# A four-stage graph network on one core: message layers written out with deeper load rings, and one scaled table between the first two layers

## What is computed

```python
h = relu(layernorm(x)); x = x + L0(h)     # conv:  relu(segment_sum((h @ W * norm)[src], dst) * norm + b)
h = relu(layernorm(x)); x = x + L1(h)     # sage:  concat([h, scaled mean of h[src] and h]) @ W1 + b
h = relu(layernorm(x)); x = x + L2(h)     # attention over edges and own edge, batch norm
h = relu(layernorm(x)); x = x + L3(h)     # three typed layers:
#   m = where(etype == 0, h @ W[0], h @ W[1])[src]
#   h = act(segment_sum(m, dst) + h @ Ws + b)      relu, relu, none
```

## Time and profile before

| | us |
|---|---|
| median of the runs (three) | 6772.4 |
| profiled execution | 6746.68 |
| its span | 6745.1 |
| conv layer (545 to 1346 us of the span) | 801 |
| sage layer (1346 to 2145) | 799 |
| attention stages (2145 to 4518) | 2373 |
| typed layers (4518 to 6745), three of 742 to 743 | 2227 |

### The profile page before, as it was taken

One profiled execution on the slowest core, in us unless ns is written; L12 is line 12 of the kernel. 1 busy time (PEld: TensorE's weight loads), 2 busy tenths in 40 slices (PEclk: granted clock), 3 DMA queues, 4 the chain that ended last, 5 costly groups with the idle time before them and its releaser, 6 DMA issues. The chain is left out here.

```text
span 6745.1 us, 89039 instructions
## 1 busy us (share of the span) xinstructions
PE 4393.0 (65%) x26272; PEld 3765.7 (56%) x26272; DVE 3539.0 (52%) x9258; ACT 2200.7 (33%) x5554; POOL 2825.2 (42%) x2867
## 2 busy tenths in 40 slices
PE   6502565546666787776659999415777477757777
PEld 5402555536655454554447777315777467656677
DVE  8862555624444565665579999762323223323333
ACT  6572544513333232232225444551111111111111
POOL 0014554255543677776500000025554455545553
PEclk9855666667777787887779999656777677777777
DMA  6033666645654222222222222343444344434444
GB/s 171 6 68 82 145 144 141 134 92 126 127 116 104 63 66 66 66 68 62 50 42 55 53 52 55 81 95 80 97 93 98 69 92 96 92 81 90 96 93 91
DMA packets 1695961, 589.73 MB, mean 87 GB/s; under 512 B 1606839, under 2 KB 1626102, under 8 KB 1695498
## 3 DMA queue, kind: packets, MB, share of 16 engines
q1 hardware_dynamic: 1189958, 380.24, 25.6%
q10 hardware_dynamic: 416196, 116.81, 7.7%
q0 software_dynamic: 89600, 90.32, 6.7%
HBM read 378.26 MB, written 222.06 MB: 89 GB/s over the span
## 5 line engine op out<-in xcount | busy, mean ns | idle before, releaser
L1944 POOL DMA_INDIRECT early<-node_g,src_w x1176 | 1141.7, 971 | 1036.1 <-DMA edge_h<-early 583.8
L1944 POOL DMA_INDIRECT l1ring<-node_g,src_w x392 | 373.5, 953 | 444.7 <-DMA edge_h<-l1ring 243.0
L1091 POOL DMA_INDIRECT fscat<-node_g,early x392 | 439.2, 1120 | 263.5 <-issue 114.3
L1206 DVE TENSOR_TENSOR fslz<-bank,fsy 128x512 f32<-128x512 f32 x448 | 267.0, 621 | 497.6 <-issue 290.9
L1944 POOL DMA_INDIRECT l0ring<-node_g,src_w x392 | 375.4, 958 | 346.2 <-DMA edge_h<-l0ring 219.8
L2604 POOL COPY x_sb<-fbxn 128x448 f32 x56 | 31.5, 562 | 1140.0 <-DVE fbxn L2663 1140.0
L1093 POOL DMA_INDIRECT fscat<-node_g,early x392 | 433.9, 1107 | 128.2 <-issue 128.2
L1182 ACT ACTIVATE fsy<-bank 128x512 f32<-128x512 f32 x448 | 242.3, 544 | 737.1 <-remote 234.6
L2021 PE MATMUL bank<-l0S,l0msg 128*128 128x128 f32 x1568 | 297.8, 366 | 146.2 <-issue 97.6
L1141 PE MATMUL bank<-Wlr,fscatT 128*128 128x256 f32 x784 | 273.1, 433 | 171.6 <-ACT fscatT L1173 147.6
L2021 PE MATMUL bank<-l1S,l1msg 128*64 128x128 f32 x1568 | 300.6, 312 | 124.8 <-issue 124.2
(11 more groups left out here) (328 smaller groups left out, 11365.2 us busy)
## 6 DMA issues: line engine op xcount, KB each, us to landing
node_g<-amax ACTq DMA_DIRECT2D x168, 224.0 KB
edge_h<-early SPq DMA_DIRECT2D x168, 224.0 KB
early<-node_g,src_w POOLq DMA_INDIRECT x1176
l0msg<-edge_a SPq DMA_DIRECT2D x56, 256.0 KB
l0msg<-edge_h SPq DMA_DIRECT2D x56, 256.0 KB
l1msg<-edge_h SPq DMA_DIRECT2D x56, 256.0 KB
alpha<-edge_h SPq DMA_DIRECT2D x56, 256.0 KB
l3win<-edge_h SPq DMA_DIRECT2D x56, 256.0 KB
```

Source lines behind the costliest of these rows:

```text
L1091: pool.indirect_dma_start(out=cat[:, s, t, 0:F], out_offset=None, in_=node_g, in_offset=bass.IndirectOffsetOnAxis(ap=src_i[:, col], axis=0 ...
L1206: v.tensor_tensor(lz[:, kind, t0:t1, :], z_bank(g)[:, 0:(t1 - t0) * HF].rearrange("p (t c) -> p t c", c=HF), y[:, g % 2, 0:t1 - t0, :], AL ...
L1944: pool.indirect_dma_start(out=ring[:, n % RING, t, :], out_offset=None, in_=table_in, in_offset=bass.IndirectOffsetOnAxis(ap=src_w[:, n * ...
```

## The change

It rewrites `layer`, and touches the plan of factors.

- Buffers: the gather ring has four slots in a typed layer (RING) and three otherwise; loaded rows have four buffers in a typed layer (DEEP) and three otherwise, instead of two. In conv and sage the ring now lies in the last third of the array `early`.
- SP's list: own rows (or edge attributes) of n + DEEP - 1 and the factors of n + 1 are asked for after the edge rows of n and the store of n + 2.
- One table between conv and sage: conv writes only the scaled rows. Sage uses them also for its own half and multiplies the product by the root that undoes the scale (`send_root`, one reciprocal at the start; one DVE operation more a window). The factors of sage are multiplied by the sending scale in the plan (`both`).
- PE, ACT and DVE are written out over the 56 windows, with one semaphore for each kind of step.
- DVE's order in a typed layer: matrices(n + 2), messages(n + 1), update(n).
- The last window gathers 6 tiles instead of 7, as the 392nd holds no edges.

The core of the diff (the waits of ACT and the index arithmetic that only follow the written-out loops are left out):

```diff
@@ plan
+                invr = tb("invr", [R, 2, NBLK * P]); both = tb("both", [P, T])
+                    pe.wait_ge(both_ok, 1)
-                        for k, of in enumerate((inv_cnt, upd_scale)):
+                        for k, of in enumerate((inv_cnt, both)):
+                    v.tensor_tensor(both[:, :], upd_scale[:, :], rs_send[:, :], ALU.mult).then_inc(both_ok, 1)
@@ layer
-                win = tb("win", [P, 2, WT, F]) if typed else None
-                msg = tb("msg", [P, 2, WT, M])
+                RING, DEEP = (4, 4) if typed else (3, 3)
+                ring = rows(ring_at, RING, HS)
+                win = rows(RING * HS * F, DEEP, WT) if typed else None
+                msg = tb("msg", [P, 2 if typed else DEEP, WT, M])
-                own = None if conv else tb("own", [P, 2, HS + 1, 2 * F if sage else F])
+                own = None if conv else tb("own", [P, DEEP, HS + 1, F])
-                RING = 3
@@ layer, gpsimd
-                        for t in range(HS):
+                        for t in range(real_tiles(n)):
@@ layer, sync
-                    def windows(n):
...
-                        if j > 0:
-                            sp.wait_ge(msg_ok[s] if typed else agg_ok[s], j)
-                            if typed:
-                                sp.wait_ge(agg_ok[s], j)
...
+                    def own_rows(n):
+                        if n >= DEEP:
+                            sp.wait_ge(agg_ok, n - DEEP + 1)
                         if conv:
...
+                        else:
+                            sp.dma_start(own[:, n % DEEP, 0:HS, :], tiles(table_in[nodes_of(n), :])).then_inc(own_in[n % DEEP], 16)
+
+                    def edge_rows(n):
+                        begin = begin_of(n)
+                        if n >= DEEP:
+                            sp.wait_ge(msg_ok if typed else agg_ok, n - DEEP + 1)
                         m = min(n + 1, NS - 1)
                         if n == 0:
                             sp.wait_ge(kept[0], 16)
                         sp.wait_ge(kept[m % RING], 16 * (m // RING + 1))
...
                     def factors(n):
+                        if n >= 2:
+                            sp.wait_ge(scaled, n - 1)
...
+                    for n in range(DEEP - 1):
+                        own_rows(n)
+                    if not typed:
+                        factors(0)
                     keep(0)
                     keep(1)
                     for n in range(NS):
+                        edge_rows(n)
                         if n + 2 < NS:
                             keep(n + 2)
-                        windows(n)
-                        if not typed and n >= 1:
-                            factors(n - 1)
-                    if not typed:
-                        factors(NS - 1)
+                        if n + DEEP - 1 < NS:
+                            own_rows(n + DEEP - 1)
+                        if not typed and n + 1 < NS:
+                            factors(n + 1)
@@ layer, tensor
                                 if sage:
-                                    nc.tensor.matmul(bank[2 * s + b][F:2 * F, col], own[:, s, t, F:2 * F], ident[:, :], start=True, stop=True)
-                                    nc.tensor.matmul(to, own[:, s, t, 0:F], ident[:, :], start=True, stop=False)
+                                    nc.tensor.matmul(bank[2 * s + b][F:2 * F, col], own[:, d, t, :], ident[:, :], start=True, stop=True)
+                                    nc.tensor.matmul(to, own[:, d, t, :], ident[:, :], start=True, stop=False)
...
+                    sums(0)
+                    for n in range(NS):
+                        if n + 1 < NS:
+                            sums(n + 1)
+                        products(n)
@@ layer, scalar
                             for t in range(HS):
-                                ins = A.activation(h[:, s, t, :], xn[:, s, t, :], ACT.Relu, bias=ln[:, s, 6, t:t + 1], scale=ln[:, s, 5, t:t + 1])
-                                if conv:
-                                    ins = A.activation(g[:, s, t, :], xn[:, s, t, :], ACT.Relu, bias=ln[:, s, 1, t:t + 1], scale=ln[:, s, 0, t:t + 1])
+                                ins = A.activation(h[:, s, t, :], xn[:, s, t, :], ACT.Relu, bias=ln[:, s, b, t:t + 1], scale=ln[:, s, m, t:t + 1])
...
-                                act.dma_start(tiles(node_h[at, :]), h[:, s, :, :]).then_inc(stored[s], 16)
-                                act.dma_start(tiles(table_out[at, :]), g[:, s, :, :]).then_inc(stored[s], 16)
+                            act.dma_start(tiles(table_out[at, :]), h[:, s, :, :]).then_inc(stored[s], 16)
@@ layer, vector
+                    if sage:
+                        v.reciprocal(send_root[:, :], rs_send[:, :])
...
+                    def messages(n):
+                        dve.wait_ge(rows_in[n % DEEP], 16 * (n // DEEP + 1))
+                        if n >= 2:
+                            dve.wait_ge(agg_ok, n - 1)
...
+                        v.tensor_tensor(o[:, s, :, :], po, wide((norm if conv else send_root)[:, tl]), ALU.mult).then_inc(o_free, 1)
+                        v.drain()
+                        v.tensor_tensor(o[:, s, :, :], o[:, s, :, :], rowb((b0 if conv else b1)[:, :]), ALU.add)
...
+                    matrices(0)
+                    matrices(1)
                     if typed:
+                        messages(0)
+                    for n in range(NS):
+                        if not typed:
+                            copied_sums(n)
+                        if n + 2 < NS:
+                            matrices(n + 2)
+                        if typed and n + 1 < NS:
+                            messages(n + 1)
+                        if typed:
+                            update(n)
+                        elif n >= 1:
+                            update(n - 1)
```

More of the change, by code:

```diff
@@ L1917, in layer @@
                 xn = lent(alpha, 2 * HS * F, lambda shape: tb("xn", shape)); h = lent(amax, 2 * HS * F, lambda shape: tb("h", shape))
-                g = tb("g", [P, 2, HS, F]) if conv else None
                 bs = tb("bs", [P, 2, HS, 6]); ln = tb("ln", [P, 2, 8, HS])
[L1920 to L1927, removed]
+                (S_ok, msg_ok, agg_ok, aT_ok, scaled, prod, o_free, x_ok, x_kept, var_ok, sd_ok, ln_ok, h_ok, padded, w_in) = (
+                    sm(n) for n in ("S_ok", "msg_ok", "agg_ok", "aT_ok", "scaled", "prod", "o_free", "x_ok", "x_kept", "var_ok", "sd_ok", "ln_ok", "h_ok", "padded", "w_in"))
+                gathered, kept = many("gathered", RING), many("kept", RING)
+                rows_in, own_in = many("rows_in", DEEP), many("own_in", DEEP)
+                inv_in, loop_out, stored = many("inv_in", 2), many("loop_out", 2), many("stored", 2)
                 PER = 16 * HS
-                RING = 3
-                rows_in = two("rows_in")
-                gathered, kept = ([sm(f"{name}{r}") for r in range(RING)] for name in ("gathered", "kept"))
-                ring = early_ring(RING) if typed else tb("ring", [P, RING, HS, F])
+                real_tiles = lambda n: min(HS, -(-N // P) - n * HS)
+                assert NS > RING and real_tiles(NS - 1) > 0
                 CH = [(0, 4), (4, HS)]
@@ L2048, in _ @@
                         pe.wait_ge(w_in, 32)
-                    sums(0, 0, True)
-                    def body(j, first, last):
-                        sums(j, 1, first)
-                        products(j, 0, first)
-                        if not last:
-                            sums(j + 1, 0, False)
-                        products(j, 1, first)
-                    body(0, True, False)
-                    with nc.tensor.Fori(1, GI - 1) as j:
-                        body(j, False, False)
-                    body(GI - 1, False, True)
+                    sums(0)
[3 more added lines that the diff above has]
+                        products(n)
                 @block.scalar
@@ L2064, in _, with evacuate @@
                     A = nc.scalar
-                    def evacuate(j, s, first):
-                        act.wait_ge(agg_ok[s], j + 1)
-                        if not first:
-                            act.wait_ge(prod[s], j)
+                    def evacuate(n):
+                        s = n % 2
+                        act.wait_ge(agg_ok, n + 1)
+                        if n >= 2:
+                            act.wait_ge(prod, n - 1)
                         r0, r1 = (F, 2 * F) if sage else (0, F if conv else 2 * F)
@@ L2089, in rows_out @@
-                        act.wait_ge(o_free[s] if typed and not final else ln_ok[s], j + 1)
-                        if not first:
-                            act.wait_ge(stored[s], 16 * n_out * j)
-                            A.sem_inc(go, 1)
-                        if norms:
+                        if not typed:
+                            act.wait_ge(x_ok, n + 1)
+                            A.copy(x_sb[:, n * HS:(n + 1) * HS, :], xn[:, s, :, :]).then_inc(x_kept, 1)
```

(23 more changed lines are left out.)

257 lines of the change are left out of this document (92 added, 165 removed).

## The result

| | before | after |
|---|---|---|
| median of the runs, us (four each) | 6765.8 (6730.6 to 6790.2) | 6975.4 (6954.4 to 7011.6) |
| profiled span | 6745.1 | 6969.2 |
| conv layer | 801 | 739.9 |
| sage layer | 799 | 817.1 |
| attention stages (code unchanged) | 2373 | 2349.9 |

The changed kernel is slower: ratio 1.034, 95% interval 1.030 to 1.037. I had said 7015 for the median (measured 6975), and 6997 for the profiled execution (measured 6969). By stages, against what was said in brackets: typed layers +291 us (+300), conv -61 (-45), sage +18 (-5), the untouched stages -23 (0).

A forecast was written before the change was run, and what follows sets the result against it. In typed layers POOL was taken to wait for SP and SP for PE, with slow stretches of unknown cause. Profiled 6746.7 + 300 (typed) - 50 (conv, sage) = 6997; 7015 as timed, range 6600 to 7370 us.

The forecast's parts named there:

- DVE's order: Typed layers: messages(n+2) now stands behind update(n) and matrices(n+3), so PE stands still 3.9 us a window before sums.
- the 0.62 us: Last typed layer: the update has a second operation of 0.62 us.
- The window: Typed window: 9.0 PE work + 3.9 standing + 1.0 slow time = 13.9 us; layer 842 against 742, +300 for three.
- The end of the slow pairs: Typed layers: POOL gathers one window and pauses, ending two-window runs with their 10 us; 1.0 us a window left.
- Loads ahead: Typed layers: deeper buffers give no earlier edge rows, as SP's list is in order; taken as 0, bounds +0.5/window, -44.3/layer.
- Conv: Conv layer: 7 of 14 activations a window and one 224 KB store go; 45 us gained, between 0 and 167.
- Sage: Sage layer: one 224 KB load less, one DVE operation and a drain more, hidden; -5 us, between -20 and +35.
- Rival A: Typed layers: slow stretches vanish and PE keeps its high clock, 10.9 us a window; 6535 us, chance 0.17.
- Rival B: Typed layers: buffers free POOL, no PE wait counts, 490 + 81 + 10 us a layer; about 5900 us, chance 0.05.
- C: Typed layers: slow pairs stay and the 3.9 us come on top, +580; 7350 us, chance 0.15.
- D: Typed layers: the 3.9 us fall into PE's present idle time, conv pays the rest; no change, 6775 us, chance 0.13.
- What would show it: PE idle 4 us before sums; DVE without pause; POOL's 7-gather runs; SP at own rows; conv's PE wait for ACT halved.

The follow-up runs named there:

- the single edit: Kernel before with only DVE's order changed, messages(n+1) instead of messages(n+2) before update(n) in typed layers: 6408 us, ratio 1.136 to the kernel before.
- the activations and the store: Two runs on the changed kernel with messages(n+2) before update(n): conv's 7 activations per window added again, 5547.8 us; its second 224 KB store added again, 5544.6 us.
- the gap filled: Changed kernel with 16 more matmuls on PE after the products of each typed window: 5943 us, ratio 1.052 to the kernel before.
- the first pair: The kernel before and the changed kernel as first measured, on a chip whose number isn't recorded: medians 6765.8 and 6975.4 us, ratio 1.034.
- the last experiment: Kernel before with PE, ACT and DVE written out over the windows instead of looping, on chip 5: 6686 us, ratio 0.999.
- the earlier trace: First profile of the unchanged kernel before, the one the prediction read: span 6745.1 us.
- the pause: Changed kernel with messages(n+2) before update(n), and POOL in typed layers waiting for a window's gathers to land before the next: 5918 us, ratio 1.049.

## Why the prediction was right, and which steps of it were not

- **DVE's order** was the step that carried the sum, and it held: 3.9 us of standing forecast, 3.89 measured in l3, and by the single edit the order makes the whole loss of the typed layers. But the standing isn't a fixed price: with 4.26, 4.61 and 5.09 us the window was 13.65 us all the same, so the 0.62 us that I expected on top in the last layer cost its windows nothing.
- **The window** of 9.0 + 3.9 + 1.0 = 13.9 us came to 9.76 + 3.89 + 0 = 13.65. Two terms were mis-sized and nearly cancelled, which is luck. I kept PE's work at 9.0 because I saw two effects on the clock and could not weigh them; the sums behind the gap run at the lower level. And I left 1.0 us of slow time where there is none. The rows to size the first were there: the same 28 matmuls in 3.34 us without a gap, against 0.186 us for one at the clock of 0.60.
- **The end of the slow pairs** was right in its effect (167 us in l3 before, none after), but I took the pattern for one of the kernel. It showed on some chips and not on others. The forecast of +300 us is therefore one for chips like the first; elsewhere the change costs 661 us. None of my cases was this one, since all took the kernel before as fixed at 6772.
- **Loads ahead** at nothing: right in the main. In the changed kernel the edge rows of a window are asked for 18.7 us before its sums (median over 40 windows), with a window of 13.65; before it was 13.8 with 12.36. That is 5 us more, not a window; how far ahead they are asked for moves with the window itself (6.9 us for the kernel before with its 8.97 us). Where the order doesn't hide it, buffers, slots and written-out code together are worth 6 to 9 us a layer, inside my bounds.
- **Conv** -61 for -45, and PE's wait for ACT fell from 75.1 to 20.5 us. The size came out near, the reason is not confirmed: on the other chips the activations and the store give back 13 and 4 us of 73. What makes the rest (both together, the third buffer and POOL's waits for a slot) is open; the loops are excluded only in so far as, written out on chip 5, conv still took 787 us and the whole kernel didn't change.
- **Sage** +18 for -5. On the other chips it is 542 against 544, so the change itself costs nothing. On the first, runs of two windows rose from 15 to 20 and the slow time from 207 to 255 us. That would explain it, but it is argued from two single traces; the untouched stages differ by 23 us as well, and in conv the same count rose by 66 us while the layer got shorter.
- **Rival A** failed on the clock, not on the slow stretches: they vanished, but PE did not stay at the high level. With the gap filled the window is near its 10.9 us (10.77). **Rival B** named its condition rightly, that messages(n+2) stand ahead of update(n): then POOL is the bound, at 533 us a layer (581 reckoned). Its price doesn't follow from its own terms: 3 x (742 - 581) + 50 off 6772 is about 6240 us, not 5900. **Rivals C and D** didn't come about: no slow pair was left, and the 3.9 us fell into no idle time.
- **What would show it**: all five signs are in the trace. One was harder to read than I said: PE's wait is listed as "issue" in the written-out code, and only the end of DVE's messages, 0.07 us before the weight load, shows the releaser.

## What to carry to other kernels

Where an engine's list is in order, look what stands between a product and the work that waits for it: moving one step of 1.3 us behind an update puts everything that stands before it on the critical path. When PE gets a new gap, look also at the matmuls behind it, which may run at the lower clock (here 3.9 us of standing and 2.9 us of slower sums), and measure the window and not the gap: gaps of 3.9 to 5.1 us made one and the same window. And don't carry a stall without a named cause into a sum as if it belonged to the kernel: bound the forecast also for the case that it isn't there.

## What the runs showed of the hardware

- The same kernel took 6766 us in the first pair, 6694 us on chip 5 and 5644 us on chips 12 and 2. In the traces the difference in the typed layers is in stretches in which PE's matmuls follow each other at 0.7 us and more while POOL gathers on (17 matmuls in 11 us in the last experiment, 6 in 8 us in the earlier trace rows). On chips of one kind they come, in the typed layers, in runs of gathers of more than one window; on the other kind POOL gathers 392 tiles in a row in a layer whose granted clock is 0.86. The cause stays open. The run made for it, the pause, fell on a chip without slow stretches.
- Behind a gap of 0.32 us in each window the 28 matmuls of the sums took 3.36 us, behind 1.04 us between 3.36 and 4.99, behind 1.96 us 4.77, behind 3.89 us 6.25. Behind still longer gaps they took less again: 5.88 us behind 4.26, 5.53 behind 4.61, 5.04 behind 5.09, in windows of 13.65 us throughout.
- 16 added f32 products in each window, whose results nothing reads, shortened the window of l3 and l4 by 2.9 us.
